# A decoder layer on one core: seven products for the down projection in the first pass too, and weight forms on GpSimd

## The reference, cut to what matters

```python
# x: (4, 512, 1024) f32; 32 heads, 8 kv heads of 32; FF = 3584
x = layernorm(x + attention(x, wq, wk, wv, wo))           # RoPE, causal
gate = x_flat @ (gate_t * gate_s[:, None]).T              # (2048, 3584)
up   = x_flat @ (up_t   * up_s[:, None]).T
out  = (silu(gate) * up) @ (down_t * down_s[:, None]).T   # (2048, 1024)
x = layernorm(x + out)
```

## Time and profile before

| | |
|---|---|
| median of three runs | 1807.24 us |
| span of the profiled execution, first to last instruction | 1801.0 us |
| PE busy | 1754.5 us, 97% |
| DVE busy | 1161.0 us, 64% |
| ACT busy | 840.3 us, 47% |
| POOL busy | 463.6 us, 26% |
| HBM read and written | 109 GB/s over the span |

### The profile page before, as it was taken

One profiled execution on the slowest core, in us unless ns is written; L12 is line 12 of the kernel. 1 busy time (PEld: TensorE's weight loads), 2 busy tenths in 40 slices (PEclk: granted clock), 3 DMA queues, 4 the chain that ended last, 5 costly groups with the idle time before them and its releaser, 6 DMA issues.

```text
span 1801.0 us, 26997 instructions
## 1 busy us (share of the span) xinstructions
PE 1754.5 (97%) x9840; PEld 844.3 (47%) x9840; DVE 1161.0 (64%) x2423; ACT 840.3 (47%) x1675; POOL 463.6 (26%) x813
## 2 busy tenths in 40 slices
PE   8999999999999989999999999999999999999998
PEld 4644555555455433444444444444444444444444
DVE  7888777667668654456544445646656766768656
ACT  6687666667566665265334343341332332232221
POOL 2455456456455552220000001202200000002203
PEclk9999999999999999999999999999999999999999
DMA  9445335235335599467635354458411111132302
GB/s 257 97 95 136 72 95 148 53 82 150 65 71 126 107 230 304 140 241 276 219 112 190 107 174 167 170 178 193 146 63 65 62 65 62 65 108 86 113 12 82
DMA packets 228852, 233.47 MB, mean 130 GB/s; under 512 B 184048, under 2 KB 184688, under 8 KB 228720
## 3 DMA queue, kind: packets, MB, share of 16 engines
q1 hardware_dynamic: 227856, 231.26, 43.5%
q10 hardware_dynamic: 864, 0.49, 0.1%
HBM read 122.78 MB, written 72.88 MB: 109 GB/s over the span
## 4 chain that ended last, share of the span: by engine, by line
PE 89%; DVE 3%; DMA 3%; POOL 1%; issue 1%; SPq 1%; ACT 1%; DVEq 0%; POOLq 0%; ACTq 0%
PE bank L1182 36%; PE bank L1067 19%; PE bank L1202 14%; PE bank L1215 7%; PE bank L1126 4%; PE bank L1109 4%; PE bank L1083 3%; PE bank L1141 1%; DMA q_stack<-stack_rows 1%; SPq L1804 1%; PE bank L1087 0%; POOL p_tiles L1684 0%; DVE bank L1433 0%; SPq L1747 0%; POOL rstd L1690 0%
## 5 line engine op out<-in xcount | busy, mean ns | idle before, releaser
L1182 PE MATMUL bank<-x_forms,weight_forms 128*128 128x512 f16 x3136 | 702.0, 379 | 6.7 <-DVE up_blocks L1595 3.1
L1182 PEld LDWEIGHTS bank<-x_forms,weight_forms 128*128 128x128 f16 x3136 | 305.6, 98 | 379.9 <-DVE up_blocks L1595 5.1
L1202 PE MATMUL bank<-down_forms 128*128 128x512 f16 (+1 forms) x1168 | 258.2, 376 | 0.0
L1274 ACT ACTIVATE p_tiles<-bank 128x512 f32<-128x512 f32 (+1 forms) x352 | 191.1, 559 | 118.1 <-PE bank L1109 116.9
L1700 POOL TENSOR_TENSOR acc<-acc,down_forms 128x1024 f32<-128x1024 f32 x16 | 39.1, 2454 | 715.9 <-DVE acc L1630 715.9
L1433 DVE CUSTOM_DVE_ANT_0 bank<-bank,cmask 128x512 f32<-128x512 f32 (+2 forms) x320 | 182.0, 601 | 59.7 <-PE bank L1083 58.0
L1067 PE MATMUL bank<-wq_parts,xT_parts 128*128 128x256 f16 x1536 | 208.6, 275 | 10.3 <-DVE wq_parts L1389 8.2
L1630 DVE TENSOR_TENSOR acc<-bank,acc 128x512 f32<-128x512 f32 x188 | 128.0, 688 | 121.3 <-PE bank L1202 64.9
L1202 PEld LDWEIGHTS bank<-down_forms 128*128 128x128 f16 x1168 | 114.1, 98 | 134.8
L1676 POOL TENSOR_SCALAR_AFFINE_SELECT p_tiles<-p_tiles 128x128 f32<-128x128 f32 (+2 forms) x352 | 128.4, 372 | 183.3 <-ACT p_tiles L1274 181.7
L1067 PEld LDWEIGHTS bank<-wq_parts,xT_parts 128*128 128x128 f16 x1536 | 148.5, 98 | 56.9 <-issue 11.0
(11 more groups left out here) (136 smaller groups left out, 2060.5 us busy)
## 6 DMA issues: line engine op xcount, KB each, us to landing
weight_forms_spill<-weight_forms SPq DMA_DIRECT2D x28, 896.0 KB, 3.8
weight_forms<-weight_forms_spill SPq DMA_DIRECT2D x28, 896.0 KB, 4.5
x_forms_spill<-x_parts SPq DMA_DIRECT2D x56, 256.0 KB, 2.5
w_page<-gateT SPq DMA_DIRECT2D x28, 512.0 KB, 5.5
w_page<-upT SPq DMA_DIRECT2D x28, 512.0 KB, 3.7
w_page<-downT SPq DMA_DIRECT2D x28, 512.0 KB, 4.3
att_spill<-att_made SPq DMA_DIRECT2D x64, 128.0 KB, 2.2
down_forms<-x_spill SPq DMA_DIRECT2D x16, 512.0 KB, 3.5
```

The lines of the kernel that those rows point to most:

```text
L1182: t = nc.tensor.matmul(strassen[bank_set(use)][to][:, :], w_form[:, use % 4, A_FORMS[a_form], k * P:(k + 1) * P], xF[:, :, B_FORMS[b_form] ...
L1202: t = nc.tensor.matmul(to[:, 0:cols.stop - cols.start], hid_p[place_of(r)][:, k, a, i // 2 * P:(i // 2 + 1) * P], wd_p[place_of(r)][:, c, ...
L1274: nc.scalar.activation(p32[j][:, h0:h0 + heads, :], bank[5 + m % 2][:, 0:heads * n].rearrange("p (h c) -> p h c", c=n), ACT.Exp, scale=SCO ...
```

## The change

1. Rounds 0 to 9 are no longer plain: `plain(n)` loses its `n < NF`. Five groups go from 16 products of 8 matmuls to 28 products of 4. The down weights of these rounds are cast straight into the place where the forms are made, and stored from there. The form T3 overwrites one of the plain blocks, so it now comes last and waits until the store to DRAM has landed; T2 is made from others than before.
2. The 112 `w_form` operations move from DVE to GpSimd.
3. The three ring buffers now hold rounds 0 to 9 in the same way as in the second pass: round r may be written once the group that contains round r-3 is done. The loads of the down scale and of x for the last additions now wait in the first pass too for the third last group before the end.
4. Durations in the planner and all of `SHIFTS` are new.

```diff
+TAIL = .12
-DOWN_MADE = ["T1", "T3", "T2", "T4"]
+DOWN_MADE = ["T1", "T2", "T4", "T3"]
-DOWNS = [(q, m) for q in range(PASSES * ND) for m in range(PAIRS * NPR if ND <= q < PASSES * ND - 1 else 2 * PT)]
+DOWNS = [(q, m) for q in range(PASSES * ND) for m in range(PAIRS * NPR if q % ND < ND - 1 else 2 * PT)]
 def plain(n):
-    return n < NF or n % NF >= PLAIN
+    return n % NF >= PLAIN
 def room_after(n):
     p, r = divmod(n, NF)
-    if p == 0:
-        return DOWN_OF[r - 4] if r > 3 else None
-    return DOWN_OF[p * NF + min(r - 3, PLAIN - 1)] if r > 2 else p * ND - 1
+    if r > 2:
+        return DOWN_OF[p * NF + min(r - 3, PLAIN - 1)]
+    return p * ND - 1 if p else None
 SHIFTS = {
-    PE: {"max_tr": -4, "pv": -2, "sums": -18},
-    SC: {..., "silu": 4, "v_copy": -8, "w_cast": 8, "x1_hi": 1},
+    PE: {"down": 15, "max_tr": -5, "product": 37, "proj_out": -12, "proj_q": 53, "pv": 30, "score_k": -26, "score_q": 7, "sums": 24},
+    SC: {..., "exp": 82, ..., "row_sum": 26, "silu": 14, ..., "w_cast": 216, "x1_hi": 36},
...
-            put(VE, at - 4 * (n >= NF), .7, "sum", n, w, k, ...)
+            put(VE, at - 4, .7, "sum", n, w, k, ...)
...
         if w < 2 and c == 1:
             for k in range(4):
-                put(VE, at + 1 + .5 * k, .45, "w_form", use, k,
+                put(PO, at + 1 + .5 * k, 1.3, "w_form", use, k,
...
+            for k, form in enumerate(DOWN_MADE * (not plain(r))):
+                put(VE, at + 8 + .5 * k, .45, "d_form", r, form, after=[("w_cast", w, r, 0), ("w_cast", w, r, 1)] + (
+                    [("d_form", r, DOWN_MADE[k - 1])] if k else []) + ([("d_store", r)] if form == "T3" else []))
...
+        def down_rows(n):
+            return wd_p[place_of(n)].rearrange("p c d -> p (c d)") if plain(n) else wd_f[n % NF % 3][:, 0:4, :].rearrange("p f c -> p (f c)")
...
 # vector_program, d_form
-                    on.wait_ge(s_din[(n - NF) % 4], 16 * din_n(n))
+                    if n >= NF:
+                        on.wait_ge(s_din[(n - NF) % 4], 16 * din_n(n))
+                    else:
+                        for c in range(2):
+                            on.wait_ge(s_cast, cast_n["w_cast", 2, n, c])
+                        if form == "T3":
+                            on.wait_ge(s_dst[n % 4], 16 * (n // 4 + 1))
...
-                                           "T2": (5, 1, 0, ALU.add), "T4": (6, 2, 5, ALU.subtract)}[form]
+                                           "T2": (5, 3, 4, ALU.subtract), "T4": (6, 2, 5, ALU.subtract)}[form]
...
 # gpsimd_program, moved from vector_program
+                elif kind == "w_form":
...
+                    nc.gpsimd.tensor_tensor(form[to], form[left], form[right], op).then_inc(s_wform, 1)
...
 # sync_program, ds_load and last_x1
-                    if which[0]:
-                        on.wait_ge(s_down, DOWN_N[DOWN_LAST[which[0] * ND + ND - 3]] + 1)
+                    on.wait_ge(s_down, DOWN_N[DOWN_LAST[which[0] * ND + ND - 3]] + 1)
```

More of the change, by code:

```diff
@@ L226 @@
 SHIFTS = {
-    PE: {"max_tr": -4, "pv": -2, "sums": -18},
[L228 to L232, removed]
+    PE: {"down": 15, "max_tr": -5, "product": 37, "proj_out": -12, "proj_q": 53, "pv": 30, "score_k": -26, "score_q": 7,
+         "sums": 24},
+    SC: {"att_hi": 1, "copy": -4, "exp": 82, "ln_exp": -9, "nat_hi": -21, "norm": -1, "row_sum": 26, "silu": 14, "split_hi": -1,
+         "v_copy": -5, "w_cast": 216, "x1_hi": 36},
+    VE: {"acc": 2, "att_scale": -127, "d_form": 61, "ds_scale": 26, "hid_form": 2, "hid_lo": 140, "hidden": 422, "ln_seed": 2,
+         "ln_step": -33, "max_copy": 19, "max_parts": -8, "norm_stats": -57, "rotate": -12, "row_max": 21, "split_lo": 6,
+         "sum": 5, "sum_turn": 92, "x1_lo": -51},
+    PO: {"causal": 4, "nat_lo": -13, "newton": 17, "presum": -2, "rope_add": -27, "w_form": -2, "x1_form": -8},
+    SY: {"att_load": -9, "bound_load": -24, "bound_store": -16, "d_in": 15, "d_store": 23, "ds_load": -21, "last_x1": 2,
+         "max_rows": 14, "out_store": -3, "page_load": 2, "row_load": -21, "stack": -24, "w_in": -9, "w_load": -1, "w_store": 17,
+         "x1_store": -20, "xF_load": 25, "xF_store": 14},
 }
@@ L389, in attention_plan @@
         if what == "out":
[L390 removed]
+            put(VE, end, 1.42, "residual", w, t, after=[made, ("row_load", w)] + stats_free(plan, len(plan.norms)))
             if t:
@@ L532, in normed @@
     if row < 2 * TILES - 1:
-        put(PO, end + 1, 2.6, "newton", row, after=[("norm_stats", row)])
+        put(PO, end + 1, 3.0, "newton", row, after=[("norm_stats", row)])
     put(SC, end + 4, 1.25, "norm", row, after=[("newton" if row < 2 * TILES - 1 else "norm_stats", row)])
@@ L556, in ffn_plan @@
             clock += NPR * one
-            for _ in range(4 if n < NF else 10):
+            for _ in range(10):
                 if left and DOWN_ROUNDS[left[0][0]][-1] < n:
                     down_at[left.pop(0)] = clock
-                    clock += one if n < NF else one / 2
+                    clock += one / 2
         while n % NF == NF - 1 and left and DOWN_ROUNDS[left[0][0]][-1] <= n:
@@ L607, in ffn_plan @@
             before = [("sum", n, w, k - 1)] if k else [("sum", *divmod(use - 1, 2), 2)] if use else []
-            put(VE, at - 4 * (n >= NF), .7, "sum", n, w, k, after=[("copy", n, w, (0, 2, 2)[k]), ended(use, (0, 4, 5)[k])] + before)
+            put(VE, at - 4, .7, "sum", n, w, k, after=[("copy", n, w, (0, 2, 2)[k]), ended(use, (0, 4, 5)[k])] + before)
         for k in range(4):
@@ L642, in ffn_plan @@
             after = [("hid_lo", r, a_form) for r in rounds]
-            after += [("d_form", r, b_form) if b_form in DOWN_MADE else ("d_in", r) for r in rounds]
+            if b_form in DOWN_MADE:
+                after += [("d_form", r, b_form) for r in rounds]
+            else:
+                after += [("d_in", r) for r in rounds] if p else [("w_cast", 2, r, c) for r in rounds for c in range(2)]
         else:
@@ L658, in ffn_plan @@
             put(PO, at + one + 1, 2.4, "scale_row", tile, after=[("acc", q, m), ("ds_scale", p)])
-            put(SY, at + one, .4, "last_x1", tile, moves=PAGE_MOVES, after=over + ([("down", *DOWN_LAST[q - 1])] if p else []) + (
+            put(SY, at + one, .4, "last_x1", tile, moves=PAGE_MOVES, after=over + [("down", *DOWN_LAST[q - 1])] + (
                 [("add_x1", tile - 1)] if tile else []))
@@ L666, in ffn_plan @@
         at = down_at[p * ND + ND - 2, 0]
-        put(SY, at, .4, "ds_load", p, moves=PAGE_MOVES, after=over + ([("down", *DOWN_LAST[p * ND + ND - 3]), ("acc", *DOWN_LAST[p * ND - 1])] if p else []))
+        put(SY, at, .4, "ds_load", p, moves=PAGE_MOVES, after=over + [("down", *DOWN_LAST[p * ND + ND - 3])] + (
+            [("acc", *DOWN_LAST[p * ND - 1])] if p else []))
         put(VE, at + 4, 1.3, "ds_scale", p, after=[("ds_load", p), ("bound", 1)])
@@ L1694, in gpsimd_program @@
                     nc.gpsimd.tensor_scalar(w, mv[:, n % 2, 0:1], r, -1.0, ALU.mult, ALU.mult).then_inc(s_newton, 1)
+                elif kind == "w_form":
+                    use, k = which
+                    form = [w_form[:, use % 4, i, :] for i in range(NPR)]
+                    for c in range(2):
+                        on.wait_ge(s_cast, cast_n["w_cast", use % 2, use // 2, c])
+                    on.wait_ge(s_wform, 4 * use + k)
+                    to, left, right, op = ((4, 2, 3, ALU.add), (5, 4, 0, ALU.subtract), (6, 1, 5, ALU.subtract),
+                                           (2, 0, 2, ALU.subtract))[k]
+                    nc.gpsimd.tensor_tensor(form[to], form[left], form[right], op).then_inc(s_wform, 1)
                 elif kind == "scale_row":
```

55 lines of the change are left out of this document (24 added, 31 removed).

## The result

The changed kernel takes 1814.28 us, the median of 5 runs (1812.99 to 1815.40). The kernel before took 1805.73 us beside it (5 runs, 1802.74 to 1810.49). The ratio is 1.0048, with a 95% interval of 1.0036 to 1.0059: slower by 8.6 us where 18 us less were predicted.

The account below looks back on a forecast made before the run. PE was taken to bound the kernel, busy for 97% of the span. The terms -17.3 + 1.0 + 1.5 + 0.5 - 4 = -18.3 us took 1807.24 to 1788.9 us, with an 8 in 10 range of 1777 to 1802.

Parts of the forecast that it names:

- Part 1: First-pass down products: 80 fewer matmuls on PE, nothing else on that path, saving 17.3 us, bounds 0 and 17.3.
- Part 3: Weight forms on GpSimd: they block DVE's two-input SBUF work, and 1.5 us of that reaches PE, bounds 0 and 11.3.
- The fourth rival: First pass: POOL forms block DVE and a quarter of 102 us reaches PE, costing 25.5 us, 1815.4 us; chance 0.05.
- in the same proportion: Upper bound for POOL forms: PE waits of 3.1 us per 39 us of POOL multiplies, scaled to 142 us, give 11.3.
- Part 4: Waits and moved steps in the first pass: 0.5 us for the store wait, 0 for the ring and later loads.
- not what it says: First pass: the ring of three stops PE between groups, so the 17.3 us are not gained, 1803 us; chance 0.05.
- The store wait: T3 waits 4.5 us for stored down weights in each of ten rounds, mostly covered by DVE's idle time: 0.5 us.
- Part 2: Ten changed rounds: DVE's net extra 59.0 us and ACT's 18.8 us fit beside the matmuls, at no cost.
- Part 5: New order of every stage, from new durations and ranks: -4 us, between +12 and -15.
- the start of the pass: Around 690 us the first GpSimd forms stand in the open and queue with layernorm steps: 1 us.
- The step from span to median: Whole kernel: the median was put 6.24 us above the profiled span, and that distance was kept in the forecast.

Follow-up runs that it names:

- `e10_slow_fills`: The kernel after, with each GpSimd weight form replaced by sixteen zero fills of 32 columns that read nothing: 1791.67 us, ratio 0.9923 to the kernel before.
- experiment 3: The kernel before with only the weight forms moved to GpSimd, plain down products and old durations and ranks kept: 1807.92 us, ratio 1.0024.
- experiments 1: The kernel after, with each GpSimd weight form replaced by zero fills that read nothing, first eight of 64 columns: 1790.23 us, ratio 0.9925 to the kernel before.
- experiments 2: The kernel after with only the weight forms put back on DVE, planned anew: 1799.61 us, ratio 0.9974 to the kernel before.
- experiment 4: The kernel before with only the seven products in the first pass, forms on DVE, old durations and `SHIFTS`: 1813.78 us, ratio 1.0055.
- experiment 5: The kernel before with only the planner's new durations and `SHIFTS`, plain down products and forms on DVE kept: 1803.93 us, ratio 0.9993.

## Why the prediction was wrong

**Part 1, the products: right.** 80 matmuls fewer, 0.86 us per product of 4. That nothing else was on their path was not: even in the best order some 10 of the 17.3 us reach the time.

**Part 3, "I take 1.5 us, bounds 0 and 11.3, close to the lower end": the step that failed.** The mechanism was named rightly, with the right rows. The additions cost 22.6 us (after against `e10_slow_fills`), fifteen times the term and twice its upper bound. Two sizes in it were off. The time DVE was held was estimated at 32 us in ten rounds and came out at 46.6 in the pass. The larger error was the share that reaches PE: 22.6 / 46.6 = 48%, where 1.5 / 32 = 5% was taken. That share was read from a DVE with room: the earlier trace rows, around 16 multiplies in 39 us. The changed stage had 18 operations per round that can be blocked instead of 7, and DVE at 73%; in the kernel before, without them, the same move held DVE for 12.0 us instead of 47.0 and cost 3.9 us (experiment 3). So the time held depends on what DVE does beside the forms, and in what order; that the share reaching PE grows with DVE's load is the likely reading of the 48%, but no run varied the load by itself. The fourth rival, slower through a blocked DVE, had this: a quarter of 102 us, 25.5 us, at a chance of 0.05. Its 1815.4 us is close to the measured 1814.3 partly by luck, since it left out the ring gap and the 2 us of attention. The price of the bound was worked out "in the same proportion"; it needed the load of the changed stage, 77% by the prediction's own sum.

**Part 4, "in the second pass, where PE lost 1.4 us. I take 0": wrong by about 8 us.** The ring of three was costed by a stage in which `acc` is free from the start. In the first pass the additions to `acc` wait for the forms of x, and so does the ring. The rival "not what it says" had named this very gap, with a time of 1803 and a chance of 0.05, and rejected it by the same row. The store wait in the same part was small, as forecast: 0.2 us of DVE for w_down_spill in `e10_slow_fills`, and none in the kernel after.

**Part 2, hidden by PE: partly wrong.** DVE's load was right (forecast 294 us without the forms; 292.67 in `e10_slow_fills`), but 112 forms of 0.42 us on the same engine cost 9.4 us (experiments 1 and 2) though DVE has idle time in sum. An engine that is 70% busy and works in order is no full cover: what counts is what stands ahead of a sum when a bank must come free. With the old order 27 us were lost (17.3 + 9.7, experiment 4), the ring gap among them. (ACT's 182.41 us is 183.92 in the earlier trace rows; nothing hangs on it.)

**Part 5, "-4 us": half.** Up to the last output projection the kernel after gains 774.0 - 766.9 = 7.1 us, of which 24 product matmuls not yet run (three products) are 5.2; 1.9 us are won. PE's idle time fell from 27.1 to 23.5 us, as forecast. Without the products the order gives nothing (experiment 5), with them 14.2 us (experiments 2 and 4); the prediction priced it once, and it has two prices.

**Part 3, the start of the pass, "1 us": about 0.** From 690 to 767 us PE idles 1.0 us in all, and no wait of PE for a form on POOL stands among its waits. In the order of the kernel before, a form on POOL was late once, by 1.3 us (experiment 3).

**The sum.** -17.3 (matmuls) - 1.9 (attention) + 22.6 (POOL additions) + 8 (ring gap) = +11.4 us, against +11.7 us between the profiled spans and +8.6 us between the medians. The 2.8 us by the medians lie within what the terms are sure to: the runs of one kernel spread by 2 to 9 us, and the ring gap is 6.7 to 10.2. The step from span to median, 6.24 us, was 1.74 in the run that was profiled; with that the forecast would have been 1784.4 us, further off.

Both rules of the Trainium skill weighed in the prediction held: the lock is in the rows, and the advice that elementwise work with two inputs belongs on VectorE (the Trainium skill, "GPSIMD Engine Reference", 4.1 Engine selection) is borne out by 14.7 us, with DVE the busier engine of the two even so. Its size was off here: 1.162 against 0.422 us is 2.8 times, where the Trainium skill says about twice.

## What to carry to other kernels

Price a blocking operation by what the blocked engine does in the changed stage, not by how rarely such blocks reached the bounding engine before. Moving two-input SBUF work from a busy DVE to POOL can cost more than it takes away (here 22 to 24 against 9 us). Fills on POOL, which only write, did not have that price, and DVE's additions with an operand in PSUM did not pay it. When a stage takes over a scheme from another stage, check what the first buffers wait for in the new place; and judge an order only together with the work that it was made for.

## What was new of the hardware

- An f16 addition of 128x512 on POOL took 1.162 us in the median (1.148 to 2.155), a little less than the f32 one at 1.272.
- DVE's scalar_tensor_tensor with both tensors in SBUF (L1622) is held up like an addition: up to 2.85 us where its median is 0.751. Fills on POOL left DVE's down forms alone, at 427 ns at most.
- The blocking goes both ways: the longest form on POOL took 2.155 us. It began at 1128.25 us, while a DVE addition with both inputs in SBUF (L1666) ran from 1127.72 to 1129.38.
- After a gap of 5.4 us in PE's work the granted clock fell to 0.75 over the following ten microseconds, and after waits of 2.4 and 0.5 us near 960 us it was 0.83 from 960 to 970 us.

The lines of the kernel after for the first of these (ns min/median/max, first and last start), the second, and the clock near 960 us:

```profile
L1720 POOL TENSOR_TENSOR weight_forms<-weight_forms x112: 1148/1162/2155, 691.2 to 1199.4; 128x512 f16<-128x512 f16 x112
...
L1622 DVE SCALAR_TENSOR_TENSOR gate_blocks<-up_blocks,up_scale,gate_blocks x84: 735/751/2846, 714.9 to 1747.4; 128x512 f32<-128x512 f32 x84
...
960.00:970.00 10.00, 9.48 (x38) 3.93 (x38) 6.43 (x10) 6.57 (x9) 2.76 (x4) 0.83 0.61 196
```
